# Shared-expert weights laid out ahead of the kernel, first rows and order table fetched early, and softmax of the routing scores moved to tiles 8 and 10

## The chip, the core and the metric

The kernel runs on one core of a Trainium2 chip. The metric is device time in microseconds (us) for one execution. The engines are TensorE (PE in the rows; PEld is its weight load), VectorE (DVE), ScalarE (ACT), GpSimd (POOL) and SyncE (SP), whose queue issues most DMAs. A granted clock of 1.00 is 2.4 GHz on TensorE, 0.5 is 1.2 GHz.

## The reference

The input is x [16, 256, 512] with a context of the same shape. The first layer multiplies the normalised x with the context in groups of 8 heads, runs a causal long convolution over the last axis, adds a skip term, multiplies with the context and sums. The second layer is a mixture of 64 experts, 6 per token, plus a shared expert.

```python
kv = vr[:, :, :, None, :] * x2r[:, :, None, :, :]
y = irfft(rfft(kv, n=2*L) * rfft(k, n=2*L))[..., :L] + kv * skip
x = x + einsum("bhijl,bhil->bhjl", y, x1r)
scores = softmax(xf @ gate_w.T)                 # xf is layernorm(x), 4096 tokens x 512
topk_w, topk_idx = top_k(scores, 6)             # each expert keeps its first 128 tokens
eo = (silu(g) * u) @ down_proj[e] * weight      # g, u = split(gx @ gate_up_proj[e])
shared = silu(xf @ sh_gate.T) * (xf @ sh_up.T) @ sh_down.T
x = x + routed + shared
```

## The kernel before

**Part A, 32 convolution tiles** (h = 0 to 31, 128 rows each). GpSimd forms the products (`product`, L1059) and their low halves (`low_part`, L1067), ScalarE the high halves (L809) and the filter blocks `toep` (L796 and L797, from `gr`, which SP loads from the DRAM tensor `filters`). TensorE convolves (`conv`, L445 to L449). VectorE multiplies the result with the context (`times`, L1221), sums it (`total`, L1227), and adds the residual (`add_x1`, L1255). Then come the second norm (`apply2` on ScalarE, L819), its transpose (`turn_xn`, L462) and the router (`router`, L468), the maximum, shifted scores and the mask of six experts (`experts_marked`, L1285; `experts_mask`, L837). These trail a tile or two behind the convolution. The transposed rows go to DRAM as `xT_rows`.

**Part B, 22 tiles of the shared expert** (t = 0 to 21). SP fetches transposed rows into `xn` (`b_load_xT`, L359), ScalarE copies them to the high half (`b_evacuate`, L903), VectorE forms the low half (`b_rows_low`, L1396). TensorE then runs two groups of 12 matmuls (`b_half`, L569: gate and up), three transposes (`b_turn_hid`, L580) and nine matmuls (`b_out`, L587). ScalarE takes the Silu (`b_gate`, L909) and evacuates the hidden rows (`b_evacuate_hid`, L915), VectorE makes `b_hidden` (L1409), `b_hidden_low` (L1401) and `b_result` (L1416). In tiles 2 to 17 VectorE also carries one round each of a search for the 128 first tokens of every expert: `first_best` (L1371) and `first_out` (L1376) over the table `place`. `place` is the DRAM constant `order` (1 MB, L389) times the turned expert masks (`places` on TensorE, L557, and `order_places` on VectorE, L1362). The weights of the first four routed experts are fetched in tiles 2 to 5.

**Part C, 64 routed experts**, with the ten remaining shared tiles spread among them. GpSimd gathers rows of `xn_rows`, whose last 64 columns are the routing probabilities, and adds results into the output.

**Handover from A to B.** The shared weights come from DRAM as they are. TensorE turns them in 11 pieces (`turn_weights`, L485 and L491), ScalarE and VectorE split each piece into high and low (L847, L1291). Four pieces stand inside the last convolution tile, seven behind it. There too stand the exponentials of all scores (L939, L945), their sums (L1445), the reciprocals and the multiplication (L1452), after which GpSimd writes the probabilities by 16 DMAs of 64 KB in pieces of 256 bytes (L1133).

Each engine runs its own instruction list in the order written. Waits are on semaphores.

## Time and profile before

| | |
|---|---|
| median of 3 runs | 1164.33 us (1163.23 to 1167.55) |
| the profiled execution | 1165.01 us, of which 1163.1 us is the span in the profile |
| TensorE busy | 1088.9 us, 94% |
| VectorE busy | 840.0 us, 72% |
| ScalarE busy | 526.9 us, 45% |
| GpSimd busy | 709.4 us, 61% |
| mean granted clock | 0.976 |

Busy shares are means over the three parts, which have different limits. The stretches matter more: A ends at about 548 us, B at about 724 us.

### The profile page before, as it was taken

To read this page: it belongs to the slowest core of one execution; us is meant where nothing else is said; L and a number is where in the kernel's file an instruction comes from. 1 tells how busy PE (TensorE), PEld (TensorE's weight loads), DVE (VectorE), ACT (ScalarE), POOL (GpSimd) and SP (SyncE) were. 2 spreads that over 40 slices of the span, in tenths; PEclk is the share of its full clock that TensorE was granted. 3 is DMA by queue.
4 is the path that set the end of the run, shared out by engine and by line. 5 is a ranking of instruction groups with operands and counts; after the bars stand their busy time and mean duration, and the time that the engine had idled before them with its cause. 6 is when DMAs were issued, how large, how long until landed. Compare 5 with 4: busy or idle time off the path is not lost. (4 is left out here: it accounts for less than half of the span.)

```text
span 1163.1 us, 17622 instructions
## 1 busy us (share of the span) xinstructions
PE 1088.9 (94%) x5113; PEld 852.8 (73%) x5113; DVE 840.0 (72%) x1444; ACT 526.9 (45%) x958; POOL 709.4 (61%) x414
## 2 busy tenths in 40 slices
PE   3999999999999999999689999999999899999973
PEld 2778777877778777787578889777777667777642
DVE  3799999999999999998579994456556455565533
ACT  5565556555665556553412222444444344444421
POOL 6999999999999999993210000154444353443623
PEclk9999999999999999999889999999999989999986
DMA  6365554455445554452485444599999999999984
GB/s 181 104 186 159 166 142 139 145 158 166 130 134 157 164 150 135 141 150 73 123 222 160 122 115 120 179 286 279 289 290 294 284 234 286 276 282 291 291 210 52
DMA packets 92029, 217.08 MB, mean 187 GB/s; under 512 B 11239, under 2 KB 16167, under 8 KB 91856
## 3 DMA queue, kind: packets, MB, share of 16 engines
q1 hardware_dynamic: 75440, 177.75, 50.3%
q0 software_dynamic: 16544, 38.78, 15.9%
q8 instruction: 22, 0.36, 0.1%
q14 instruction: 23, 0.19, 0.0%
HBM read 164.82 MB, written 52.18 MB: 187 GB/s over the span
## 5 line engine op out<-in xcount | busy, mean ns | idle before, releaser
L1059 POOL TENSOR_TENSOR ring<-vT,pT 128x1024 f32<-128x1024 f32 x128 | 249.1, 1956 | 9.5 <-ACT vT L803 9.5
L445 PE MATMUL Y<-split,toep 128*128 128x512 f32 x576 | 238.4, 414 | 11.5 <-ACT toep L797 9.4
L1067 POOL TENSOR_TENSOR split<-ring,split 128x1024 fp32r<-128x1024 f32 x96 | 230.8, 2404 | 1.6 <-ACT split L809 1.6
L447 PE MATMUL Y<-split,toep 128*128 128x512 f32 x576 | 227.4, 395 | 0.0
L446 PE MATMUL Y<-split,toep 128*128 128x512 f32 x576 | 226.2, 393 | 0.0
L689 PE MATMUL Y<-ring,xT 128*128 128x384 f32 x512 | 193.1, 501 | 0.8 <-DMA ring<-in_L_ffn_down_proj_dram 0.8
L1221 DVE TENSOR_TENSOR z<-Y,cT 128x1024 f32<-128x1024 f32 x128 | 157.0, 1227 | 26.5 <-PE Y L449 25.4
L1106 POOL DMA_INDIRECT stage<-xn_rows,idx_i x64 | 75.7, 1183 | 161.9 <-issue 161.6
L1227 DVE TENSOR_REDUCE o<-z 128x128 f32<-128x1152 f32 x128 | 172.2, 1345 | 1.2
L445 PEld LDWEIGHTS Y<-split,toep 128*128 128x128 f32 x576 | 109.1, 189 | 31.6 <-issue 10.3
L809 ACT ACTIVATE split<-ring 128x1024 fp32r<-128x1024 f32 x96 | 100.8, 1050 | 57.9 <-POOL ring L1059 57.9
L447 PEld LDWEIGHTS Y<-split,toep 128*128 128x128 f32 x576 | 108.7, 189 | 24.2
L446 PEld LDWEIGHTS Y<-split,toep 128*128 128x128 f32 x576 | 109.4, 190 | 19.8 <-issue 0.5
L689 PEld LDWEIGHTS Y<-ring,xT 128*128 128x128 f32 x512 | 88.9, 194 | 39.9 <-issue 2.1
L569 PE MATMUL Y<-split 128*128 128x384 f32 x528 | 105.4, 349 | 4.5 <-DVE split L1291 4.5
L569 PEld LDWEIGHTS Y<-split 128*128 128x128 f32 x528 | 95.4, 195 | 6.7 <-DVE split L1291 3.1
L1516 DVE TENSOR_TENSOR split<-TB,split 96x256 fp32r<-96x256 f32 x64 | 26.9, 420 | 100.6 <-ACT split L1004 98.8
L1127 POOL DMA_INDIRECT out_dram<-o,idx_i x16 | 25.9, 1617 | 106.2 <-DVE o L1561 55.3
L1127 POOL DMA_INDIRECT out_dram<-w,idx_i x16 | 25.7, 1606 | 99.3 <-DVE w L1561 38.8
L986 ACT ACTIVATE xT<-TA 128x512 f32<-128x512 f32 x64 | 37.6, 588 | 68.4 <-PE TA L677 68.4
L449 PE MATMUL Y<-ring,toep 128*128 128x512 f32 x128 | 65.3, 591 | 0.0
L903 ACT ACTIVATE split<-xn 128x512 fp32r<-128x512 f32 x32 | 20.2, 631 | 82.8 <-DMA xn<-xT_rows 76.7
(167 smaller groups left out, 1905.1 us busy)
## 6 DMA issues: line engine op xcount, KB each, us to landing
ring<-_L_ffn_gate_up_proj_dram SPq DMA_DIRECT2D x64, 768.0 KB, 6.8
ring<-in_L_ffn_down_proj_dram SPq DMA_DIRECT2D x64, 384.0 KB, 8.9
gr<-filters SPq DMA_DIRECT2D x32, 512.0 KB, 4.0
stage<-in_x_dram SPq DMA_DIRECT2D x32, 256.0 KB, 5.4
pT<-in_turned_dram SPq DMA_DIRECT2D x32, 256.0 KB, 4.2
cT<-in_turned_dram SPq DMA_DIRECT2D x32, 256.0 KB, 4.2
xr<-in_x_dram SPq DMA_DIRECT2D x32, 256.0 KB, 3.7
xn_rows<-xn SPq DMA_DIRECT2D x32, 256.0 KB, 2.9
```

Of the source, the lines that this page charges most:

```text
L445: pe.matmul(y, high, kv[:, s, 0, a, n], start=(a == 0), stop=False)
L446: pe.matmul(y, high, kv[:, s, 1, a, n], start=False, stop=False)
L447: last = pe.matmul(y, low, kv[:, s, 0, a, n], start=False, stop=(a == c))
L449: last = pe.matmul(y, toep0[:, s, :], kv3[s][:, n], start=False, stop=True)
L569: last = pe.matmul(Y[2 * s + g][:, 0:SI], xTs[:, s, a, c, :], sh_gu[:, b, c, g * SI:(g + 1) * SI], start=(c + a + b == 0), stop=(c == NC - ...
L689: last = pe.matmul(Y[s][:, 0:SI], xT[:, s, c, :], ring[:, r, c * SI:(c + 1) * SI], start=(c == 0), stop=(c == NC - 1))
L809: act.activation(kv[:, s, 0, c, :], kvp[c], ACT.Copy).then_inc(kv_high, 1)
L1059: pool.tensor_tensor(to.rearrange("p (b j i) -> p b j i", i=NH, j=NH), a, d, ALU.mult).then_inc(kvp_ready, 1)
L1067: pool.tensor_tensor(kv[:, s, 1, c, :], kvp[c], kv[:, s, 0, c, :].bitcast(F32), ALU.subtract).then_inc(kv_ready, 1)
L1106: pool.indirect_dma_start(out=xg[r], out_offset=None, in_=xn_rows, in_offset=bass.IndirectOffsetOnAxis(ap=idx_i[:, e:e + 1], axis=0),).the ...
L1221: dve.tensor_tensor(zz[c % 2][:, :, :, 0:NH], YY[c % 2][:, :].rearrange("p (b j i) -> p b j i", j=NH, i=NH), m, ALU.mult).then_inc(z_done, 1)
L1227: dve.tensor_reduce(o[:, s, c, :], z[:, c % 2, :].rearrange("p (n i) -> p n i", i=NH + 1), AX.X, ALU.add).then_inc(o_done, 1)
```

## The change

1. **Weights laid out.** The host function `shared_rows` lays the three shared matrices out in the transposed order. The 11 turns on TensorE are gone, with the 11 ScalarE and 11 VectorE pieces. In their place ScalarE makes three copies of 128x1536 (`shared_high`), GpSimd two subtractions of 128x1536 after its last product, and VectorE one (`shared_down_low`).
2. **First rows and order early.** Rows of tiles 0 and 1 of B go into `pT`, free after the last product, and not into `xn`. The order table is issued before the last stores. `places` writes TA and DX, no longer OT and DX. TensorE runs three tiles' halves while the last tile's norm, router and mask proceed.
3. **Other first instructions.** SP issues x first and `load_filter(0)` ahead of four tile transfers. ScalarE takes a square root of a constant first.
4. **Softmax later.** One exponential over all scores stands on ScalarE after tile 8, between two loops. The sums and the multiplication stand on VectorE in tile 10, which carries no round of the search. The search thus ends in tile 18.

```diff
+GATE_AT = 10
...
+        PL = [TA, DX]
...
+        shared = [ring[:, n, 0:n_up * L] for n in range(3)]
+        shared_to = [[sh_gu[:, a, :, g * SI:(g + 1) * SI] for a in range(2)] for g in range(2)]
+        shared_to.append([sh_d[:, a, :, :] for a in range(2)])
+
+        def shared_from(n):
+
+            return shared[n].rearrange("p (c i) -> p c i", c=n_up if n == 2 else NC)
+
+        def b_rows(t, s):
+
+            return pT[:, s, :, :].rearrange("p c n -> p (c n)") if among(t, 0, 1) else xn[:, s, :]
...
+            load_rows(0, 0)
             sp.dma_start(kin, k).then_inc(k_in, 16)
-            load_rows(0, 0)
             sp.dma_start(sq[:], c_sq).then_inc(consts_in, 16)
+            load_paired(0, 0)
+            sp.dma_start(skip_c[:].rearrange("p h i -> p (h i)"), bass.AP(skip.tensor, skip.offset, [[0, P], [1, D]])).then_inc(skip_in, 16)
             sp.dma_start(gate_in[:], gate_w).then_inc(gate_w_in, 16)
-            sp.dma_start(skip_c[:].rearrange("p h i -> p (h i)"), bass.AP(skip.tensor, skip.offset, [[0, P], [1, D]])).then_inc(skip_in, 16)
             sp.wait_ge(k_high, 1)
             sp.wait_ge(k_low, 1)
             for part in range(2):
                 sp.dma_start(filters[:, part, :], kparts[part].bitcast(F32)).then_inc(filters_out, 16)
             sp.dma_start(filters[:, 2, :], kpad).then_inc(filters_out, 16)
-            load_paired(0, 0)
             load_turned(0, 0)
             load_rows(1, 1)
+            sp.wait_ge(filters_out, 48)
+            load_filter(0)
             load_paired(1, 1)
             load_turned(1, 1)
             load_residual(0, 0)
             load_residual(1, 1)
             sp.dma_start(slot_c[:], c_slot).then_inc(small_in, 16)
-            sp.wait_ge(filters_out, 48)
-            load_filter(0)
...
+            sp.dma_start(shared[0], shared_rows[0]).then_inc(shared_in, 16)
...
                 if among(t, 0, 1):
-                    sp.wait_ge(xT_ps, NT - 1 + t)
+                    sp.wait_ge(kvp_ready, (NT - 1 + t) * NC)
+                elif among(t, 2, 3):
+                    sp.wait_ge(xT_ps, NT - 3 + t)
                     sp.wait_ge(xn_out[s], NT // 2 * 16)
                 else:
                     sp.wait_ge(b_xT_lo, t - 1)
                 sp.wait_ge(xT_out[s], landed(t, s, 16))
-                sp.dma_start(xn[:, s, :], xT_rows[t]).then_inc(b_xT_in[s], 16)
+                sp.dma_start(b_rows(t, s), xT_rows[t]).then_inc(b_first_in[s] if among(t, 0, 1) else b_xT_in[s], 16)
...
+            for t in range(2):
+                b_load_xT(t, t)
             store_xT(NT - 2, 0)
-            b_load_xT(0, 0)
+            b_load_xT(2, 0)
+            sp.wait_ge(z_done, NC * NT)
+            sp.wait_ge(o_done, NC * NT)
+            sp.dma_start(place, c_order).then_inc(order_in, 16)
             store(NT - 1, 1, late=True)
-            b_load_xT(1, 1)
             for t in range(2):
                 b_load_x1(t, t)
             store_xT(NT - 1, 1)
+            b_load_xT(3, 1)
...
+            b_iteration(0, 0, fetch_xT=False)
+            b_iteration(1, 1, fetch_xT=False)
+            sp.wait_ge(sh_lo, 2)
+            sp.wait_ge(sh_d_lo, 1)
...
-                else:
-                    pe.wait_ge(term_ready, NT)
-                    pe.wait_ge(xT_sb, NT - 2)
-                    turn_weights(0)
...
-                if among(h, NT - 1):
-                    turn_weights(1)
...
+                    last = pe.matmul(PL[g % 2][:, n * P:(n + 1) * P], mask[:, 2 * m:2 * m + 2, :], ident16[:],
...
-            for n in range(4, 7):
-                turn_weights(n)
-            turn_weights(7)
+            pe.wait_ge(z_done, NC * NT - 1)
+            pe.wait_ge(b_xT_lo, 1)
+            pe.wait_ge(sh_lo, 1)
+            b_half(0, 0, 0)
             turn_o(NT - 1, 1)
-            turn_weights(8)
-            pe.wait_ge(b_xT_lo, 1)
-            pe.wait_ge(sh_lo, 2 * NC)
-            b_half(0, 0, 0)
+            pe.wait_ge(sh_lo, 2)
+            b_half(0, 0, 1)
+            pe.wait_ge(z_done, NC * NT)
+            pe.wait_ge(b_xT_lo, 2)
+            b_half(1, 1, 0)
             pe.wait_ge(xT_sb, NT - 1)
             turn_xn(NT - 1, 1)
-            b_half(0, 0, 1)
+            b_half(1, 1, 1)
             pe.wait_ge(sc_ready, NT - 1)
             router(NT - 1, 1)
-            turn_weights(9)
-            turn_weights(10)
+            b_turn_hid(0, 0)
+            pe.wait_ge(b_xT_lo, 3)
+            pe.wait_ge(b_hid, 1)
+            b_half(2, 0, 0)
             places(0)
             places(1)
-            pe.wait_ge(b_xT_lo, 2)
-            b_half(1, 1, 0)
+            pe.wait_ge(x1_ready, NT)
+            pe.wait_ge(sh_d_lo, 1)
+            b_out(0, 0)
+            b_turn_hid(1, 1)
+            b_half(2, 0, 1)
             places(2)
-            b_turn_hid(0, 0)
-            pe.wait_ge(sh_lo, n_turn)
-            b_half(1, 1, 1)
             places(3)
-            pe.wait_ge(place_sb, 3)
-            b_out(0, 0)
-            b_iteration(2, 0)
+            pe.wait_ge(place_sb, 4)
+            b_out(1, 1)
             with pe.Fori(0, 9) as i:
...
+            act.wait_ge(dve_setup, 2)
+            act.activation(sd2[:], eps[:], ACT.Sqrt)
...
                 if n == 0:
+                    act.wait_ge(shared_in, 48)
                     act.wait_ge(conv_done, NC * (NT - 1))
-                if n == 2 * NC:
-                    act.wait_ge(conv_done, NC * NT)
-                act.activation(part[:, 0, :], bank, ACT.Copy).then_inc(w_sb, 1)
+                act.activation(shared_to[n][0], shared_from(n), ACT.Copy).then_inc(sh_hi, 1)
...
-            for n in range(3, 7):
-                shared_high(n)
             act.wait_ge(conv_done, NC * NT)
             b_evacuate(0, 0)
-            shared_high(7)
+            b_evacuate(1, 1)
+            keep_scores(NT - 2)
             sqrt2(NT - 1)
             apply2(NT - 1, 1)
-            keep_scores(NT - 2)
-            shared_high(8)
+            experts_mask(NT - 2)
             evacuate_xn(NT - 1, 1)
-            experts_mask(NT - 2)
-
-            act.wait_ge(sc_kept, NT - 1)
-            most, last = sc_all[:, 0:NT - 1, :], sc_all[:, NT - 1:NT, :]
-            act.activation(most, most, ACT.Exp).then_inc(exp_ready, 1)
-            b_evacuate(1, 1)
-            shared_high(9)
+            b_gate(0, 0)
+            b_gate(1, 1)
             keep_scores(NT - 1)
             experts_mask(NT - 1)
-            act.wait_ge(sc_kept, NT)
-            act.activation(last, last, ACT.Exp).then_inc(exp_ready, 1)
-            b_gate(0, 0)
-            shared_high(10)
             b_evacuate(2, 0)
             b_evacuate_hid(0, 0)
-            b_gate(1, 1)
             b_iteration(2, 0)
-            with act.Fori(0, NB // 2 - 2) as i:
+            with act.Fori(0, 3) as i:
+                b_iteration(i * 2 + 3, 1)
+                b_iteration(i * 2 + 4, 0)
+            act.wait_ge(sc_kept, NT)
+            act.activation(sc_all[:], sc_all[:], ACT.Exp).then_inc(exp_ready, 1)
+            with act.Fori(3, NB // 2 - 2) as i:
                 b_iteration(i * 2 + 3, 1)
                 b_iteration(i * 2 + 4, 0)
             b_iteration(NB - 1, 1)
...
+            for n in range(2):
+                pool.wait_ge(sh_hi, n + 1)
+                pool.tensor_tensor(shared_to[n][1], shared_from(n), shared_to[n][0].bitcast(F32),
+                                   ALU.subtract).then_inc(sh_lo, 1)
...
-                else:
-                    shared_low(0)
...
-                if not nxt:
-                    shared_low(1)
...
+            b_rows_low(0, 0)
             best_logit(NT - 2)
             total(NT - 1, 1, 3)
             scores(NT - 2)
-            for n in range(4, 7):
-                shared_low(n)
-            b_rows_low(0, 0)
-            shared_low(7)
+            b_rows_low(1, 1)
             add_x1(NT - 1, 1)
-            best_scores(NT - 2)
             stats2(NT - 1, 1)
             mean2(NT - 1)
+            best_scores(NT - 2)
+            six_scores(NT - 2)
             rstd2(NT - 1)
-            six_scores(NT - 2)
             shift2(NT - 1)
             experts_marked(NT - 2)
-            shared_low(8)
+            shared_down_low()
+            b_hidden(0, 0)
             best_logit(NT - 1)
             scores(NT - 1)
             best_scores(NT - 1)
             six_scores(NT - 1)
             experts_marked(NT - 1)
-            b_rows_low(1, 1)
-            shared_low(9)
-
-            dve.wait_ge(exp_ready, 2)
-            dve.tensor_reduce(sums[:], sc_all[:], AX.X, ALU.add).then_inc(sums_ready, 1)
-            dve.wait_ge(sums_ready, 1)
-            dve.reciprocal(rinv[:], sums[:]).then_inc(rinv_ready, 1)
+            b_rows_low(2, 0)
+            b_hidden(1, 1)
+            b_hidden_low(0, 0)
             order_places(0)
-            b_hidden(0, 0)
             order_places(1)
-            dve.wait_ge(rinv_ready, 1)
-            dve.tensor_tensor(sc_all[:], sc_all[:], rinv[:].unsqueeze(2).to_broadcast([P, NT, E]),
-                              ALU.mult).then_inc(prob_ready, 1)
-            shared_low(10)
-            b_rows_low(2, 0)
+            b_result(0, 0)
             order_places(2)
-            b_hidden_low(0, 0)
             order_places(3)
-            b_hidden(1, 1)
-            b_result(0, 0)
...
+                if among(t, GATE_AT):
+                    gate_sums()
...
+                if among(t, GATE_AT):
+                    gate_weights()
...
-            for n in range(NF):
-                b_iteration(n + 2, n % 2, n)
-            for t in range(MOVE_AT, NB):
-                b_iteration(t, t % 2)
+            for t in range(2, NB):
+                n = t - 2 - (t > GATE_AT)
+                b_iteration(t, t % 2, n if t != GATE_AT and n < NF else None)
...
+    up_parts = [a.reshape(SI, P, NC).transpose(1, 2, 0).reshape(P, NC * SI) for a in (gate, up)]
+    down_part = down.T.reshape(SI // P, P, L).transpose(1, 0, 2).reshape(P, SI // P * L)
+    return np.stack(up_parts + [down_part])
```

The first place is SP's queue at the start. `stage` is x, `z` the filter's input k, `pT` and `cT` two copies of the context, `xr` the residual. Before:

```order
L278 DMA z<-in_L_xattn_k_dram 32x512
L255 DMA stage<-in_x_dram 128x1x512
L280 DMA sq<-in_sq_dram 128x256
L281 DMA gate_in<-in_L_ffn_gate_w_dram 64x512
L282 DMA skip_c<-in_fside_S_0_dram 128x256
L286 DMA filters<-split 32x640 x2
L287 DMA filters<-z 32x640
L265 DMA pT<-in_turned_dram 128x512
L260 DMA cT<-in_turned_dram 128x512
...
L276 DMA xr<-in_x_dram 128x1x512 x2
L295 DMA slot_c<-in_slot_dram 128x1
L270 DMA gr<-filters 128x2x512
```

The same queue after the change:

```order
L260 DMA stage<-in_x_dram 128x1x512
L284 DMA z<-in_L_xattn_k_dram 32x512
L285 DMA sq<-in_sq_dram 128x256
L270 DMA pT<-in_turned_dram 128x512
L287 DMA skip_c<-in_fside_S_0_dram 128x256
L288 DMA gate_in<-in_L_ffn_gate_w_dram 64x512
L292 DMA filters<-split 32x640 x2
L293 DMA filters<-z 32x640
L265 DMA cT<-in_turned_dram 128x512
L260 DMA stage<-in_x_dram 128x1x512
L275 DMA gr<-filters 128x2x512
```

The load of `gr` moved ahead of `pT`, `cT` and both `xr`, and `pT` of tile 0 ahead of the filter stores.

The second place is TensorE from the last router of part A to the first `b_out`. `Y0` and `Y1` are the two-bank PSUM tiles, `xT` and `gateT` belong to the router. Before:

```order
L468 MATMUL DX<-gateT,xT 128x64 x4
L485 MATMUL Y0<-sq,ring 128x128 x6
L485 MATMUL TB<-sq,ring 128x128 x3
L485 MATMUL Y1<-sq,ring 128x128 x3
L456 MATMUL OT<-sq,o 128x128 x4
L491 MATMUL Y1<-sq,ring 128x128 x4
L569 MATMUL Y0<-split 128x384 x12
L462 MATMUL TA<-sq,xn 128x128 x4
L569 MATMUL Y0<-split 128x384 x12
L468 MATMUL DX<-gateT,xT 128x64 x4
...
L587 MATMUL OT<-split 128x512 x9
```

After the change:

```order
L475 MATMUL DX<-gateT,xT 128x64 x4
L539 MATMUL Y0<-split 128x384 x12
L463 MATMUL OT<-sq,o 128x128 x4
L539 MATMUL Y0<-split 128x384 x12
L539 MATMUL Y1<-split 128x384 x12
L469 MATMUL TA<-sq,xn 128x128 x4
L539 MATMUL Y1<-split 128x384 x12
L475 MATMUL DX<-gateT,xT 128x64 x4
L550 MATMUL TB<-sq,cT 128x128 x3
L539 MATMUL Y0<-split 128x384 x12
...
L557 MATMUL OT<-split 128x512 x9
```

The seven weight turns are gone, and four halves stand ahead of the second router where there were two.

The third place is ScalarE after tile 8, where the second loop of part B begins (`split<-xn` is `b_evacuate`, `vT<-Y` is `b_gate`, `split<-TB` is `b_evacuate_hid`). After the change:

```order
L915 ACT_TABLE_LOAD
L915 ACTIVATE sc_all<-sc_all 128x2048 [waits sc_kept]
L916 UNCONDITIONAL_BRANCH
L916 ISA
L873 REGISTER_ALU [waits b_xT_in0]
L874 ACT_TABLE_LOAD
L874 ACTIVATE split<-xn 128x512 [waits up_ps]
L877 REGISTER_ALU
L880 ACT_TABLE_LOAD [waits b_hid]
L880 ACTIVATE vT<-Y 128x384 [waits gate_ps]
L885 REGISTER_ALU [waits b_hT_ps]
L886 ACTIVATE split<-TB 128x384 [waits b_down]
```

Two loads of the activation tables now stand inside the body of the second loop, which runs seven times (two tiles each). The loop of the kernel before has none.

## Rows read from the trace of the kernel before

**Rows 1.** Windows: us, busy PE PEld DVE ACT POOL, PEclk, DMA share, GB/s
```profile
548.00:588.00 40.00, 28.06 (x159) 25.15 (x159) 26.30 (x46) 15.07 (x27) 10.78 (x16) 0.87 0.47 114
...
622.00:698.00 76.00, 74.04 (x398) 67.52 (x397) 71.71 (x76) 16.37 (x33) 0.00 (x0) 1.00 0.41 114
...
724.00:1163.00 439.00, 404.56 (x1784) 292.52 (x1783) 227.19 (x418) 174.69 (x328) 186.30 (x138) 0.96 0.91 254
```

**Rows 2.** Timeline of the start: start us, us, engine, operation, [idle before, releaser]
```profile
6.63 1.28 ACT L785 ACT_TABLE_LOAD   x1
...
11.39 3.85 POOL L1059 TENSOR_TENSOR ring<-vT,pT 128x1024 f32<-128x1024 f32 x2 [0.91 <-ACT vT L803]
...
18.75 0.31 ACT L796 ACTIVATE toep<-gr 128x128 f32<-128x128 f32 x1 [3.62 <-DMA gr<-filters]
...
21.10 2.37 POOL L1067 TENSOR_TENSOR split<-ring,split 128x1024 fp32r<-128x1024 f32 x1 [1.65 <-ACT split L809]
...
29.01 0.50 PE L445 MATMUL Y<-split,toep 128*128 128x512 f32 x1 [1.39 <-POOL split L1067]
```

**Rows 3.** Timeline of TensorE, routers that end tiles 29, 30 and 31
```profile
513.89 1.00 PE L468 MATMUL DX<-gateT,xT 128*128 128x64 f32 x8
...
530.23 1.00 PE L468 MATMUL DX<-gateT,xT 128*128 128x64 f32 x8
...
547.62 1.00 PE L468 MATMUL DX<-gateT,xT 128*128 128x64 f32 x8
```

**Rows 4.** Timeline of the handover from A to B
```profile
547.82 1.23 DVE L1221 TENSOR_TENSOR z<-Y,cT 128x1024 f32<-128x1024 f32 x1 [1.43 <-PE Y L449]
...
553.00 0.68 DVE L1255 TENSOR_TENSOR stage<-OT,xr 128x512 f32<-128x512 f32 x1
...
553.23 2.35 PE L569 MATMUL Y<-split 128*128 128x384 f32 x12 [1.65 <-DVE split L1291]
...
555.57 1.29 ACT L819 ACTIVATE xn<-stage,nb,rs 128x512 f32<-128x512 f32 x1 [0.48 <-DVE nb L1212]
...
559.55 1.00 PE L468 MATMUL DX<-gateT,xT 128*128 128x64 f32 x8
...
562.08 0.21 DVE L1285 MATCH_REPLACE8 marked<-s,sc 128x66 f32<-128x66 f32 x1
...
564.46 3.64 PE L569 MATMUL Y<-split 128*128 128x384 f32 x12
...
570.34 0.69 DVE L1362 TENSOR_TENSOR z<-z,OT 128x512 f32<-128x512 f32 x1 [3.24 <-DMA z<-in_order_dram]
...
585.77 2.24 PE L587 MATMUL DX<-split 128*128 128x512 f32 x9
```

**Rows 5.** Timeline of tiles 2 to 6 of part B
```profile
592.71 0.63 ACT L903 ACTIVATE split<-xn 128x512 fp32r<-128x512 f32 x1 [8.28 <-DMA xn<-xT_rows]
...
596.87 4.18 PE L587 MATMUL OT<-split 128*128 128x512 f32 x9 [4.33 <-DVE split L1401]
...
606.20 2.24 PE L587 MATMUL DX<-split 128*128 128x512 f32 x9
...
619.96 2.21 PE L587 MATMUL DX<-split 128*128 128x512 f32 x9
```

**Rows 6.** Timeline: the exponentials' table load, and a steady tile of B
```profile
558.43 1.28 ACT L939 ACT_TABLE_LOAD   x1
...
559.72 1.86 ACT L939 ACTIVATE sc_all<-sc_all 128x1984 f32<-128x1984 f32 x1
...
621.80 0.63 ACT L903 ACTIVATE split<-xn 128x512 fp32r<-128x512 f32 x1 [3.19 <-DMA xn<-xT_rows]
...
623.55 0.68 DVE L1396 TENSOR_TENSOR split<-xn,split 128x512 fp32r<-128x512 f32 x1
```

**Rows 7.** GpSimd's low parts (groups by line), and its DMAs' share in 545 to 615 us
```profile
L1067 POOL TENSOR_TENSOR split<-ring,split 128x1024 fp32r<-128x1024 f32 x96 | 230.8, 2404 | 1.6 <-ACT split L809 1.6
...
q0 software_dynamic: 768, 1.07, 12.7%
```

110 lines of the change are left out of this document (33 added, 77 removed).

## Prediction

> **What bounds the kernel now.** I read the page first, then the windows by stage, then the timeline at the seams. In part B's steady stretch TensorE is busy 74.0 of 76 us and VectorE 71.7 of 76 [rows 1]: TensorE paces it, VectorE is 3% behind. In part C the DMA engines are 91% busy at 254 GB/s [rows 1]. That stage starts when the token list is there, so whatever is saved before it moves it forward one for one. The poor stretch is 548 to 588 us: TensorE is busy 28.1 of 40 us, at a granted clock of 0.87 [rows 1]. The timeline says why. TensorE's first half of part B starts at 553.23, behind weight turns; the adder of the last residual, ready behind VectorE's weight pieces, runs at 553.00; the order table holds VectorE until 570.34, where its queue, `b_hidden` included, stands behind `order_places` [rows 4]. I call the end of the last convolution e = 547.8 (VectorE's last `times` starts at 547.82). The second `b_out` ends at 585.77 + 2.24 = 588.0, which is e + 40.2 [rows 4].
>
> **The start, -2.7 us.** GpSimd's chain sets it: TensorE waits at 29.01 for GpSimd's third low part [rows 2]. Two things leave that chain. The table load of 1.28 us ahead of the first product goes to time zero, but the filter's input k now lands behind x and the constant's square root stands ahead, for which I give back 0.3: -1.0. GpSimd's wait of 1.65 us at 21.10 was on a ScalarE copy, which stood behind a wait of 3.62 us for the filter load [rows 2]. That load now goes ahead of four transfers, so the wait should vanish: -1.65. Queued behind SP's earlier wait on the filter stores are `pT` and `cT` of tile 1, both residuals and tile 2, all needed a tile later. Bounds: -0.5 (x and k late) to -4.9 (1.28 + 3.62, if everything follows ScalarE).
>
> **Tile 31, -1.8 us.** Routers start at 513.89, 530.23 and 547.62: a usual tile takes 16.34, the last 17.39 [rows 3], although it turns no next tile. The four weight turns fill that. Without them I expect about 15.6, since the missing turn of v is worth some 0.7 of the 16.34. Bounds: -1.0 (VectorE becomes the later one) to -2.4. The three new ScalarE copies stand where six waits on TensorE stood. GpSimd's two subtractions cost 3.6 us each (2.404 us for 1024 columns [rows 7], times 1.5). They are covered by its idle time: behind its last low part it has nothing but the 16 DMA issues (10.78 us [rows 1]). Uncovered, they would hold the second half until e + 7.2, some 2 us.
>
> **The handover, -9.7 us.** Followed by row durations from e. `times` 1.23 and `b_rows_low` 0.68 end at e + 1.9 (tile 0's rows are fetched while tile 31 runs). The half of 2.35 us ends at e + 4.3. Turning o, two halves, turning the normed rows, one half and the router come to some 9.5 (three halves of 2.35, three short groups of 0.6 to 1.0): e + 13.8. Beside it runs the norm: from 553.00 to 555.57 + 1.29 it took 3.9 us [rows 4], so rows that are added at e + 5.1 are normed at e + 9.0, before TensorE asks. From the router's end (559.55 + 1.00) to the marks (562.08 + 0.21) there were 1.7 us. Now ScalarE's mask, its copy for tile 2 (0.63) and `b_rows_low` (0.68) follow, so the next half starts at e + 17.2. That is a TensorE gap of some 2.5 us, after a turn of the hidden rows. After such a gap the half took 3.64 us instead of 2.35, and the nine matmuls at 596.87, after 4.33 us of waiting, 4.18 instead of 2.21 [rows 4, 5], so I charge 3.64: e + 20.9. `places` twice 0.8, `b_out` 2.24, turn and half 3.0, `places` with two multiplications of 0.69 in turn 1.4, `b_out` 2.24: e + 30.5 against 40.2. The order table is issued at e + 3.5 and had 8 us to land before; it is needed at e + 21. Bounds: -5 (one more wait of the size of VectorE's 3.24 us for that table, with its clock loss) to -13 (no gap).
>
> **Tiles 2 to 5, -5.2 us.** Between 588.0 and the `b_out` that ends at 619.96 + 2.21 = 622.2 lie four tiles in 34.2 us. Steady, two tiles take 619.96 - 606.20 = 13.76, so four 27.5 [rows 5]. The excess is the 8.28 us wait for rows fetched at 592.71 and its echo [rows 5]. That fetch met the weights of the first routed experts and GpSimd's probability writes, which filled 12.7% of 70 us of the 16 engines, 8.9 us [rows 7]. The writes are gone from there, the weights not: I allow 1.5 us, 29.0. Bounds: 0 (the weights did it) to -6.7.
>
> **What is added, +3.0 us.** (a) The search ends a tile later, 17 loaded tiles for 16. TensorE lacks 76 - 74.04 us over 11 tiles, 0.2 each [rows 1], and the tile with sums and multiplication carries a reciprocal besides: together 0.5. The list is still made in tile 21. (b) The 8.9 us of probability writes now meet tile 10's transfers. Bounds 0 to 8 (two late fetches of 4 us). The load there is only 114 GB/s [rows 1], so I take 1.5. (c) The exponential, 1.28 + some 1.9 us [rows 6], fits ScalarE's 3.19 us of waiting for rows at 621.80. (d) The order of the changed kernel shows two table loads inside the second loop, seven passes, 14 loads of 1.28 us. The first stands behind the wait for the rows. In a steady tile the copy would end at 621.80 + 1.28 + 0.63 = 623.71, VectorE took it at 623.55 [rows 6]: 0.2 us late in the five passes with search, 1.0 in all. The second lies between copy and Silu, where ScalarE waits for TensorE. Without that cover: 2.56 less the slack of 623.55 - 622.43 = 1.1, seven times, 10 us.
>
> The Trainium skill, "ScalarE: Activation LUTs", section "What ACT_TABLE_LOAD costs", puts a switch at 1283 ns of load plus about 1380 ns of drain, 2.66 us. The row shows the load's 1.28, with the exponential starting right behind it at 559.72 [rows 6]. By the page's figure the copy would come 1.5 us late in seven passes, an estimate of 11 us, and the sum would end near 1158; I go by the row.
>
> **Sum.** -2.7 - 1.8 - 9.7 - 5.2 + 3.0 = -16.4. Against the profiled execution (1163.1 of span plus 1.9 around it, 1165.0) that gives 1148.6; the median of the runs stands 0.7 lower: 1147.9, rounded to 1148.
>
> **Rivals.**
> - *The handover keeps a wait* (0.09). The late fetches, the mask or a subtraction holds TensorE once more, with clock loss. For it: every wait there is on a chain of four engines. Against: nothing long is ahead of `b_hidden` now. Handover and tiles 2 to 5 then bring half, 7.5 less: 1155.
> - *More than forecast* (0.08): no low clock, no cost of the writes, full gain at the start: 1148 less 13, 1131 to 1139.
> - *Table loads on the path* (0.06): 10 us, less the 1.0 in the sum: 1157. The drain of the page would act so.
> - *Slower* (0.03): the same loads, and TensorE falls to the low clock in each of the seven passes. Then each costs 1.4 + 1.97 (4.18 less 2.21) + 1.29 (3.64 less 2.35) = 4.7 us, 33 in all: 1180. It decides from 2.5 us per pass (17.4 over 7). Against it: the steady clock is 1.00 and the loads' gap is 0.2 us by the rows.
> - *No effect* (0.02): the gain is given back before part C, for instance by a token list held by the probabilities; they are written some 80 us before it.
>
> **How the numbers follow.** The forecast holds 0.72, within 1139 to 1157 by the terms' bounds when not all fall on one side; with parts of the first and third rival the range holds 0.8. About 0.5% (5.8 us) is what a measurement of this kernel tells from no change. Faster: 0.72 + 0.09 + 0.08 + 0.03 = 0.92. Same: 0.03 + 0.02 = 0.05. Slower: 0.03.
>
> **What would show it.** Start: TensorE's wait for the third low part ends near 26.3, none of GpSimd's on ScalarE's second copy. Last router some 15.6 after the one before, e near 543.3. Second `b_out` ended by e + 31, its successors 6.9 apart, no wait of 4 us on rows. In tiles 9 to 21 VectorE's `b_rows_low` waits 0.2 us on ScalarE every second tile; waits of over 1 us there would make me wrong, as would late fetches in tile 10 for longer than two tiles, or a gap of over 5 us ahead of the third half.

## The result, and the profile after

The changed kernel takes 1161.66 us (median of 20 runs, 1156.45 to 1164.32); the kernel before takes 1164.88 in the same job (20 runs, 1162.47 to 1171.65). The ratio of the two is 0.9953, with a 95% interval of 0.9937 to 0.9968. It is faster by 3.2 us in the medians and 5.5 in the ratio, where 17 were forecast: the direction was right, the size was not, and 1161.66 lies above the range. The profiled execution spans 1161.0 us, against 1163.1 before.

The windows, which answer to [rows 1], show the handover denser and the steady stretch of part B thinner. Part C follows; its loss is taken up at the end. Columns as in [rows 1].

```profile
546.00:586.00 40.00, 32.72 (x176) 29.82 (x177) 26.66 (x43) 9.97 (x19) 0.00 (x0) 0.91 0.53 163
622.00:698.00 76.00, 68.61 (x358) 62.21 (x357) 64.35 (x68) 27.11 (x40) 10.79 (x16) 0.98 0.47 117
715.00:1161.00 446.00, 407.20 (x1785) 293.71 (x1783) 227.24 (x418) 175.10 (x328) 188.11 (x138) 0.95 0.90 250
```

In the 40 us of the handover TensorE is busy 32.7 instead of 28.1 us. In 622 to 698 it is busy 68.6 of 76 instead of 74.0. That is where an added cost sits that the forecast had put too low.

The timelines of the start and of the last routers answer to [rows 2, 3]. TensorE's wait for the third low part ends at 26.73 instead of 29.01, and tile 31 takes 543.82 - 527.98 = 15.84 instead of 17.39.

```profile
18.84 2.37 POOL L1031 TENSOR_TENSOR split<-ring,split 128x1024 fp32r<-128x1024 f32 x1
...
26.73 0.50 PE L452 MATMUL Y<-split,toep 128*128 128x512 f32 x1 [2.44 <-POOL split L1031]
...
527.98 1.00 PE L475 MATMUL DX<-gateT,xT 128*128 128x64 f32 x8
...
543.82 1.00 PE L475 MATMUL DX<-gateT,xT 128*128 128x64 f32 x8
```

The handover answers to [rows 4]; e is now 544.02.

```profile
545.94 2.33 PE L539 MATMUL Y<-split 128*128 128x384 f32 x12 [1.12 <-DVE z L1189]
...
555.37 1.00 PE L475 MATMUL DX<-gateT,xT 128*128 128x64 f32 x8
...
559.69 3.77 PE L539 MATMUL Y<-split 128*128 128x384 f32 x12 [2.62 <-DVE split L1355]
...
563.89 2.33 PE L557 MATMUL OT<-split 128*128 128x512 f32 x9
...
573.60 3.88 PE L557 MATMUL DX<-split 128*128 128x512 f32 x9 [4.51 <-DVE split L1360]
```

The first half ends at e + 4.3, the router at e + 12.4 (forecast e + 13.8), and behind it comes the gap of 2.6 us with tile 2's half of 3.77, which ends at e + 19.4 (forecast e + 20.9). What was not forecast is the last row. The second `b_out` waits 4.51 us and ends at e + 33.5, not e + 30.5. VectorE says what it waits for:

```profile
569.52 0.68 DVE L1321 TENSOR_TENSOR z<-z,DX 128x512 f32<-128x512 f32 x1
570.12 0.69 DVE L1355 TENSOR_TENSOR split<-xn,split 128x512 fp32r<-128x512 f32 x1
570.72 2.29 DVE L1330 MAX8 w<-z 128x8 f32<-128x2048 f32 x1
572.92 0.54 DVE L1360 TENSOR_TENSOR split<-TB,split 128x384 fp32r<-128x384 f32 x1
```

`b_hidden_low(1)` (L1360) takes what ScalarE copied from 566.58 to 567.07, 5.9 us before it starts, but stands behind the last `order_places`, tile 3's rows and the first MAX8.

The rows of tiles 13 and 14 come late. ScalarE's copy waits 6.78 and then 7.62 us for them, where [rows 6] had 3.19, beside the 16 probability writes on GpSimd. TensorE then waits behind VectorE, ahead of the `b_out` of tiles 11 and 12 (the expectations below call them 10 and 11):

```profile
643.25 0.63 ACT L874 ACTIVATE split<-xn 128x512 fp32r<-128x512 f32 x1 [6.78 <-DMA xn<-xT_rows]
...
652.26 1.28 ACT L874 ACT_TABLE_LOAD   x1 [7.62 <-DMA xn<-xT_rows]
653.55 0.63 ACT L874 ACTIVATE split<-xn 128x512 fp32r<-128x512 f32 x1
...
634.58 10.79 POOL L1101 DMA_DIRECT2D xn_rows<-sc_all  x16 [95.95 <-DVE sc_all L1418]
...
647.42 2.31 PE L557 MATMUL DX<-split 128*128 128x512 f32 x9 [2.74 <-DVE split L1360]
...
657.72 2.89 PE L557 MATMUL OT<-split 128*128 128x512 f32 x9 [3.46 <-DVE split L1360]
```

**One table for all profiles.** Each kernel below left one profile. The columns are differences of start times on VectorE: `b_result` of tile 1, then from tile 1 to 5, 5 to 9, 9 to 13 and 13 to 21, then the start of `b_result(21)`. After that comes part C, from the first expert's `c_hidden` to the last one's, and in it the stretch from expert 29 to 33. The last column is the median of all runs of that kernel. The kernels ran in six jobs, and the kernel before had medians from 1164.48 to 1165.92 in them; each kernel's ratio is to the kernel before of its own job. So two versions are better compared by the difference of their ratios (0.001 is 1.2 us) than by their medians, and their intervals are 2 to 4 us to either side.

```
kernel           y1      1-5    5-9    9-13   13-21  y21     C       29-33  median
before           588.76  34.19  27.52  27.49  51.51  729.47  402.94  34.28  1164.88
before_again     588.30  34.06  27.52  27.49  51.48  728.85  406.08  37.25  1164.93
smalladd_before  587.59  31.26  30.66  27.51  51.48  728.50  383.46  24.95  1147.55
after            577.52  28.21  27.96  35.26  51.62  720.57  409.26  39.19  1161.66
after_again      578.22  28.87  28.19  35.72  51.58  722.58  410.06  39.43  1162.25
delay8           577.58  28.43  27.99  34.24  51.51  719.75  407.21  37.67  1166.82
delay21          575.97  27.72  28.02  33.06  51.78  716.55  408.95  37.84  1181.70
smalladd_after   577.92  30.62  28.40  33.43  51.99  722.36  386.50  24.77  1146.23
oldstart         580.62  30.99  28.28  36.00  51.54  727.43  403.77  35.49  1160.36
early            578.54  34.17  27.52  27.51  51.58  719.32  403.67  33.64  1158.75
peel             577.96  28.26  27.46  33.23  51.47  718.38  404.76  35.91  1157.47
hidlow           574.74  27.90  27.74  33.81  51.76  715.95  402.04  32.79  1155.75
peel_hid         574.96  32.23  27.44  34.07  51.52  720.22  404.72  34.57  1154.65
spread           579.31  27.87  28.14  30.30  60.59  726.21  403.90  35.13  1162.46
twice            579.41  27.92  28.16  36.83  56.68  729.00  414.09  37.35  1165.25
spwrites         577.60  28.82  27.80  29.36  55.48  719.06  410.76  40.54  1159.13
hid_all          576.57  31.95  30.88  35.81  53.85  729.06  407.28  39.33  1163.32
best             576.41  28.95  27.46  27.94  52.40  713.16  403.13  33.06  1149.13
best_all         576.23  27.79  29.11  27.39  51.27  711.79  404.75  35.25  1150.93
```

The first three rows run the same part B as the kernel before, the next five that of the changed kernel. Their means give what the change does up to the end of part B: y1 588.22 to 577.44 (-10.8), tiles 1 to 5 33.17 to 28.77 (-4.4), 5 to 9 -0.5, 9 to 13 27.50 to 34.34 (+6.8), 13 to 21 +0.2, in all 728.94 to 720.36, -8.6. One of the three traces of part B before (smalladd_before) has its late row behind tile 5 and not ahead of it. Against the two others alone tiles 1 to 5 give -5.4 and tiles 5 to 9 +0.6, with the same sum. So 8.6 of the forecast 16.4 are there when part C starts, and 3.2 to 5.5 at the end.

### The profile page after: what moved, and what is told of

The parts are those of the page before. It is cut to its first block and busy times, and to the rows that moved or that the text cites. A ratio compares the mean times of both kernels' runs of the same rounds, so it can differ in the third digit from the quotient of the medians.

```text
span 1161.0 us, 17543 instructions
## 1 busy us (share of the span) xinstructions
PE 1086.6 (94%) x5077; PEld 849.0 (73%) x5077; DVE 836.5 (72%) x1434; ACT 541.0 (47%) x961; POOL 718.2 (62%) x416
## 5 line engine op out<-in xcount | busy, mean ns | idle before, releaser
L659 PE MATMUL Y<-ring,xT 128*128 128x384 f32 x512 | 196.0, 507 | 0.4 <-DMA ring<-in_L_ffn_down_proj_dram 0.4
L659 PEld LDWEIGHTS Y<-ring,xT 128*128 128x128 f32 x512 | 90.4, 197 | 40.5 <-issue 4.2
L1101 POOL DMA_DIRECT2D xn_rows<-sc_all x16 | 10.8, 717 | 96.0 <-DVE sc_all L1418 96.0
```

Source lines behind the costliest of these rows:

```text
L659: last = pe.matmul(Y[s][:, 0:SI], xT[:, s, c, :], ring[:, r, c * SI:(c + 1) * SI], start=(c == 0), stop=(c == NC - 1))
```

## The experiments

### What part C does with an earlier or later start

**delay8** puts additions on GpSimd ahead of the first gather:

```diff
+            for n in range(7):
+                pool.tensor_tensor(w[:, 0, :], zeros[:, 0:L], zeros[:, 0:L], ALU.add).then_inc(delayed, 1)
+                pool.wait_ge(delayed, n + 1)
             for e in range(NG - 2):
                 fetch(e)
```

> The changed kernel with seven additions of 128 x 512 zeros on GpSimd between the token list and the first gather of part C, some 8 us by GpSimd's rate in this trace (2.404 us for 1024 columns). Theory A (part C absorbs an earlier start: it is held by its transfers from about expert 30 on, so a later start costs less than itself): the first gather moves by about 8, the end by only 2 to 4 us, so the time is 1164 to 1166. Rival B (part C starts when the list is there and every us ahead of it counts; that the gain of the changed kernel vanished at experts 30 and 60 is chance): the end moves by 8, the time is about 1169 to 1170.

Measured: 1166.82 us, 5.2 above the changed kernel's median; the ratio to the kernel before is 1.0008 (0.9985 to 1.0031), 0.0055 or 6.4 us above that of the changed kernel. In the trace the first gather comes 7.8 us later than `b_result(21)` would have it, and the first expert 6.5. The medians lie between the two theories, the ratio near B. So the lever was made longer.

**delay21** is the same with `range(21)`.

> The changed kernel with 21 additions instead of 7 ahead of the first gather of part C: 21.0 us by the 7.0 that the seven took. Theory A (part C absorbs): the time rises by less than 17, below 1179. Theory B (one for one, the rest is chance in the stalls near experts 30 and 60): the time rises by 21 plus some 0.5 for a low clock behind the wait, to 1181 to 1184.

Measured: 1181.70 us, 20.0 above; ratio 1.0144 (1.0112 to 1.0176), 22.3 above the changed kernel's.

```profile
709.93 23.70 POOL L1109 TENSOR_TENSOR w<-zeros 128x512 f32<-128x512 f32 x21 [66.54 <-DVE idx_i L1355]
734.57 1.07 POOL L1075 DMA_INDIRECT stage<-xn_rows,idx_i  x1 [0.94 <-POOL w L1109]
```

The additions take 23.7 us, not 21, so the first expert is some 23 us late and the kernel 20 to 22 (the changed kernel in the same job, after_again below: 1162.25). Theory A falls: part C does not give a shifted start back. Of the forecast's premise the part "moves it forward one for one" holds.

**before_again** and **after_again** are second profiles of the two kernels, unchanged.

> The kernel before once more, for a second profile of it. Theory A (the stalls of part C are chance): from its first gather to the last expert part C takes anything between 415 and 423 us, as in six profiles of changed versions. Rival B (part C of the changed kernel is slower by itself, by some 3 to 4 us): it takes 416 again, and its stall near expert 60 stays at 37.9, below all those of the changed versions (38.5 to 40.7).

> The changed kernel once more, for a second profile of it. By chance in part C: it takes 415 to 422 us from the first gather to the last expert instead of the first profile's 423.0; the first gather lies between 714 and 717; the profiled span is 1152 to 1160. If part C of this kernel is slower by itself, it takes 422 to 424 again.

Measured: 1164.93 us, ratio 0.9990 (0.9973 to 1.0007), for the first; 1162.25, ratio 0.9959 (0.9930 to 0.9988), for the second. From first gather to last expert before_again takes 419.2 us and after_again 423.2, against 416.1 and 423.0 in the first profiles. The kernel before thus varies by 3 us, as chance would have it; the changed one repeated its long value, against what I expected of chance. Its first gather (716.8) was as expected, its span (1163.2) was not. Experts 0 to 29 take 175.6 to 175.7 us in 16 of the 19 profiles; the differences arise near experts 30 and 60.

**smalladd_before** and **smalladd_after** cut the accumulated tiles of part C to 8 of 128 rows:

```diff
-                    pool.dma_start(rows(out[0:T, :], t), y2[(t - NB) % NY2], accum_op=ALU.add).then_inc(y2_added, 16)
+                    pool.dma_start(rows(out[0:T, :], t)[0:1], y2[(t - NB) % NY2][0:NH], accum_op=ALU.add).then_inc(y2_added, 16)
```

> The kernel before with each of the ten accumulated tiles of part C (256 KB from GpSimd's queue) cut to 8 of its 128 rows, so that the output of those tiles lacks the shared experts in the other rows. Theory A (these two bursts of five tiles are what stalls TensorE near experts 30 and 60, and the stalls vary from run to run and hide the changed kernel's gain): the stall of 13 to 18 us between two c_out near expert 30 vanishes, the kernel ends 5 to 12 us earlier, and the changed kernel cut in the same way ends 8 to 9 us ahead of this one, as its first gather does. Rival B (part C as a whole runs at the rate of its transfers): the difference of the two stays near 3 us.

> The changed kernel cut in the same way (8 of 128 rows of each accumulated tile, the shared experts are missing from the other rows). Theory A: 8 to 9 us ahead of the kernel before cut so. Rival B: 3 us ahead, and TensorE waits for gathers or weights in other places of part C instead.

Measured: 1147.55 and 1146.23 us, ratios 0.9855 (0.9829 to 0.9881) and 0.9850 (0.9818 to 0.9882). Experts 29 to 33 take 24.8 to 25.0 us instead of 32.8 to 40.5, so the burst of five accumulated tiles is what stalls them. In the whole kernel the wait is VectorE's, for the adds of an earlier pair that queue behind the burst. Before ("o<-DX" is the copy of an expert's result):

```profile
929.45 0.69 DVE L1547 COPY o<-DX 128x512 f32<-128x512 f32 x1 [6.65 <-DMA out_dram<-o,idx_b]
```

After:

```profile
924.96 0.69 DVE L1509 COPY o<-DX 128x512 f32<-128x512 f32 x1 [10.49 <-DMA out_dram<-o,idx_b]
```

The second half of theory A was not confirmed: cut, the changed kernel is 1.3 us ahead in the medians, with intervals wide enough for 0 and for 5; in the profiled pair the spans are 1146.2 and 1141.0. Even with the burst cut, part C of the changed kernel is 3.0 us longer (386.50 against 383.46), nearly all of it in the last five experts.

### The start

**oldstart** undoes the first instructions only (cut to its core):

```diff
-            act.wait_ge(dve_setup, 2)
-            act.activation(sd2[:], eps[:], ACT.Sqrt)
...
-            load_rows(0, 0)
             sp.dma_start(kin, k).then_inc(k_in, 16)
+            load_rows(0, 0)
...
             sp.dma_start(slot_c[:], c_slot).then_inc(small_in, 16)
+            sp.wait_ge(filters_out, 48)
+            load_filter(0)
```

> The changed kernel with SyncE's and ScalarE's first instructions as before: k ahead of x, the filter load behind the loads of tile 1 and both residuals, no square root of the constant first. By the term of the forecast and the traces TensorE's wait for the third low part ends at 29.0 instead of 26.7, the first gather comes 2.3 us later (717 to 719), and the time is about 2.3 higher than the changed kernel's in the same job.

Measured: TensorE's wait for the third low part ends at 29.52 us, 2.8 and 2.4 later than in the two profiles of the changed kernel (26.73, 27.11), and GpSimd's wait on ScalarE is back:

```profile
21.63 2.37 POOL L1029 TENSOR_TENSOR split<-ring,split 128x1024 fp32r<-128x1024 f32 x1 [2.32 <-ACT split L779]
...
29.52 0.50 PE L452 MATMUL Y<-split,toep 128*128 128x512 f32 x1 [2.29 <-POOL split L1029]
```

`b_result(1)` comes 3.2 us later than the mean. The median, 1160.36, ratio 0.9962 (0.9943 to 0.9981), does not show it: the changed kernel in the same job has 1162.25 and 0.9959, and a shift of 2.4 us is below what these intervals tell. The expected 2.3 us in the time were not seen; those in the trace were.

### The handover

**hidlow** moves the low part of tile 1's turned hidden rows ahead of the first MAX8:

```diff
-                if first is not None:
+                if first is not None and not among(t, 2):
                     first_best(first)
...
                 b_hidden_low(t - 1, 1 - s)
+                if among(t, 2):
+                    first_best(first)
```

> The changed kernel with VectorE's low part of tile 1's turned hidden rows ahead of the first MAX8 search round instead of behind it. Theory: TensorE's wait of 4.51 us before the second b_out (573.60) shrinks by the 2.29 us of the MAX8, and the second b_out ends at e + 31, the first gather comes 2 to 3.5 us earlier. Rival (VectorE is behind anyway, and the MAX8 round only moves): b_out of tile 1 is earlier but tile 2's hidden rows are later by the same, and nothing is left at the fifth b_out.

Measured: 1155.75 us, ratio 0.9922 (0.9894 to 0.9950): 5.9 us below the changed kernel in the medians, 3.6 in the ratios. The wait falls from 4.51 to 2.32 us. The granted clock over the nine matmuls is 1.00 instead of 0.54, and they take 2.32 instead of 3.88.

```profile
570.05 2.32 PE L557 MATMUL DX<-split 128*128 128x512 f32 x9 [2.32 <-DVE split L1360]
```

Against the means y1 is 2.7 us earlier and `b_result(5)` 3.6, so the gain is kept in this trace, and the theory stands for the wait. It is not kept in every trace: peel_hid and best (below) carry the same edit, and there a later row is late in tiles 2 to 5, so that `b_result(5)` comes at 607.2 and 605.4, where the means of the changed kernel give 606.2.

**hid_all** does the same in every tile:

```diff
-                if first is not None:
-                    first_best(first)
...
                 b_hidden_low(t - 1, 1 - s)
+                if first is not None:
+                    first_best(first)
```

> The changed kernel with the low part of the turned hidden rows ahead of the MAX8 in every tile, not only in tile 2. Theory (a late row costs TensorE 2.3 us more than its lateness, because MAX8 stands between the row's low part and the hidden rows' low part, so the probability writes and table loads are dear only through that order): b_result 9 to 13 falls from 33 to 37 us to 29 to 32, the first gather comes at 706 to 709, time 1150 to 1154. Rival (hidden_low now waits for ScalarE's copy and holds MAX8 back, VectorE becomes the bound): steady tiles take more than 6.9 us, b_result 5 to 9 more than 28.5, time above 1158.

Measured: 1163.32 us, ratio 0.9996 (0.9972 to 1.0019), and 9 to 13 takes 35.81. The theory falls, and what the rival named is there: tiles 5 to 9 take 30.88 us, and the first of them, 8.59 us, ends before the table load of the exponential. MAX8 now stands behind two waits on ScalarE, and in every second tile of the second loop the copy of the hidden rows comes a table load after the copy of the rows as well.

```profile
658.48 0.63 ACT L874 ACTIVATE split<-xn 128x512 fp32r<-128x512 f32 x1
659.12 1.28 ACT L880 ACT_TABLE_LOAD   x1
660.42 0.49 ACT L880 ACTIVATE vT<-Y 128x384 f32<-128x384 f32 x1
660.81 0.48 ACT L886 ACTIVATE split<-TB 128x384 fp32r<-128x384 f32 x1
```

### What was added in part B

**peel** writes ScalarE's tiles 9 and 10 out behind the exponential:

```diff
-            with act.Fori(3, NB // 2 - 2) as i:
+            b_iteration(9, 1)
+            b_iteration(10, 0)
+            with act.Fori(4, NB // 2 - 2) as i:
```

> The changed kernel with ScalarE's tiles 9 and 10 of part B written out behind the exponential, so that the loop over the later tiles starts with the table it needs and holds no table load. Theory A (the 14 loads of 1.28 us are hidden but for the first copy after the probability writes): the first gather comes 0.5 to 2 us earlier. Rival B (the loads are what tiles 9 to 21 lost): the first gather comes 4 us or more earlier, and b_out of tile 10 and 11 no longer waits 2.7 and 3.5 us on VectorE.

Measured: 1157.47 us, ratio 0.9939 (0.9918 to 0.9960). In the trace the first gather comes 2.2 us earlier and the two late tiles stay, against rival B:

```profile
646.94 2.31 PE L557 MATMUL DX<-split 128*128 128x512 f32 x9 [2.32 <-DVE split L1362]
655.67 3.88 PE L557 MATMUL OT<-split 128*128 128x512 f32 x9 [1.89 <-DVE split L1362]
```

By the traces of peel and peel_hid tiles 9 to 13 take 33.65 instead of 34.34 us and 13 to 21 51.50 instead of 51.70: the loads cost 0.9 us, less than tiles 9 to 21 differ between traces of the changed kernel (84.8 to 87.3). The median is 4.2 lower, but the ratio only 1.6 us, which is within the intervals. The Trainium skill's figure ("ScalarE: Activation LUTs", section "What ACT_TABLE_LOAD costs"), by which the forecast had them at an estimate of 11 us, is not borne out: the rows of hid_all above show a load of 1.28 us that starts right behind the copy (658.48 + 0.63, load at 659.12), and the next instruction right behind the load (660.42).

**twice** issues the 16 probability writes a second time in tile 15:

```diff
-            for b in range(B):
...
+            for again in range(2):
+                if again:
+                    pool.wait_ge(prob_out, B * 16)
+                    pool.wait_ge(y_ready, GATE_AT + 5)
+                for b in range(B):
...
-            pool.wait_ge(prob_out, B * 16)
+            pool.wait_ge(prob_out, 2 * B * 16)
```

> The changed kernel with the 16 probability writes issued a second time in tile 15. Theory A (a burst of these writes makes the rows of two tiles late and costs some 5 us): the waits of 2 to 3.5 us on VectorE behind tiles 10 and 11 come again behind tiles 15 and 16, the first gather is 4 to 6 us later, the time 1165 to 1168. Rival B (the two late tiles come from the ends of the exponential and of the sums): no new wait, the time stays at 1162.

Measured: 1165.25 us, ratio 1.0000 (0.9983 to 1.0017), and tiles 13 to 21 take 56.68 instead of 51.70 us: one burst costs 5.0 (15 of its writes from 680.2 on, the last at 697.9), and the ratio is 5.5 us above that of the changed kernel. The profiled run is this kernel's slowest, 1175.83; its further excess sits in part C (414.09). Two tiles are late, one of them at a granted clock of 0.53 (3.88 us instead of 2.3):

```profile
692.14 3.88 PE L557 MATMUL OT<-split 128*128 128x512 f32 x9 [2.24 <-DVE split L1364]
701.97 2.31 PE L557 MATMUL DX<-split 128*128 128x512 f32 x9 [1.41 <-DVE split L1364]
```

**early** puts exponential, sums and gate weights back to the front, and with them the writes:

```diff
-GATE_AT = 10
+GATE_AT = 2
...
-            b_iteration(2, 0)
-            with act.Fori(0, 3) as i:
-                b_iteration(i * 2 + 3, 1)
-                b_iteration(i * 2 + 4, 0)
             act.wait_ge(sc_kept, NT)
             act.activation(sc_all[:], sc_all[:], ACT.Exp).then_inc(exp_ready, 1)
-            with act.Fori(3, NB // 2 - 2) as i:
+            b_iteration(2, 0)
+            with act.Fori(0, NB // 2 - 2) as i:
```

> The changed kernel with its second half undone: the exponential behind tile 1, sums and gate weights in tile 2, so that the search runs from tile 3 on, the probability writes meet the weights of the first experts as before, and the second loop has no table load. Theory A (the writes cost 6 to 7 us where they now stand, in tiles 9 to 13, and less beside the experts' weights, where rows were late anyway): b_result 9 to 13 takes 27.5 instead of 33 to 37 us, 1 to 5 to 5 to 9 together gains or loses at most 4, the second b_out comes 0 to 3 us later, and the time is 1157 to 1161. Rival B (moving them away was worth the 5.2 us and more that were forecast): tiles 2 to 5 take 34 us again, the second b_out comes 4 us later, the time is 1164 or more.

Measured: 1158.75 us, ratio 0.9951 (0.9934 to 0.9969). Tiles 1 to 5 take 34.17 instead of 28.77 us (+5.4), tiles 9 to 13 27.51 instead of 34.34 (-6.8), y1 is 1.1 later, and y21 is 1.0 earlier. Neither theory holds whole. Theory A has the time and tiles 9 to 13, but tiles 1 to 9 together lose 4.8 us where it allowed 4; rival B has tiles 2 to 5 at 34 us again, but not the 1164. The second half of the change thus moved a cost of 5 to 7 us from one place to another, and no gain is left of it (the ratios differ by 0.2 us, with an interval of some 3 to either side). In the front it looks just as in the later place:

```profile
589.76 0.63 ACT L874 ACTIVATE split<-xn 128x512 fp32r<-128x512 f32 x1 [7.27 <-DMA xn<-xT_rows]
...
577.65 10.78 POOL L1098 DMA_DIRECT2D xn_rows<-sc_all  x16 [38.53 <-DVE sc_all L1415]
```

**spread** issues the writes two at a time from GpSimd, a pair for each finished tile:

```diff
             for b in range(B):
+                if b and b % 2 == 0:
+                    pool.wait_ge(y_ready, GATE_AT + b // 2)
```

> The changed kernel with the 16 probability writes on GpSimd issued two at a time, one pair for each finished tile from tile 10 on, not all at once. Theory A (the burst of small writes makes the two fetches of rows for tiles 11 and 12 late, 7 to 8 us instead of 4, and that is most of the 7.7 us that tiles 6 to 21 lost, where 3.0 were forecast): TensorE's waits of 2.74 and 3.46 us behind tiles 10 and 11 vanish and the first gather comes 5 to 7 us earlier. Rival B (the table loads did it): the waits stay, the first gather moves by less than 1 us.

Measured: 1162.46 us, ratio 0.9983 (0.9960 to 1.0005). The two waits are gone, but four others of 1.7 to 2.5 us stand behind every second tile, and tiles 9 to 21 take 90.9 us against 86.0. Theory A holds for the two tiles and fails for the sum: spread over tiles with a table load, the same writes cost more. The fetches of rows land 5.2 us after their issue (median in 650 to 710 us), where they took 3.8 in the steady tiles of the kernel before.

**spwrites** lets SyncE issue them, behind the transfers of tiles 11 to 18:

```diff
-            with sp.Fori((2 + NW) // 2, MOVE_AT // 2) as i:
+            with sp.Fori((2 + NW) // 2, GATE_AT // 2) as i:
...
-            for t in range(MOVE_AT, NB):
+            for t in range(GATE_AT, NB):
...
+                if GATE_AT < t <= GATE_AT + B // 2:
+                    sp.wait_ge(prob_ready, 1)
+                    for b in range(2 * (t - GATE_AT) - 2, 2 * (t - GATE_AT)):
+                        sp.dma_start(xn_rows[b * D:(b + 1) * D, L:].rearrange("(h j) e -> j h e", j=NH),
+                                     sc_all[b * NH:(b + 1) * NH, :, :]).then_inc(prob_out, 16)
...
-            for b in range(B):
-                pool.dma_start(xn_rows[b * D:(b + 1) * D, L:].rearrange("(h j) e -> j h e", j=NH),
-                               sc_all[b * NH:(b + 1) * NH, :, :]).then_inc(prob_out, 16)
```

> The changed kernel with the probability writes issued by SyncE, two behind the transfers of each of tiles 11 to 18, in the queue of the rows and not on GpSimd's. Theory A (the fetches of rows are late because the small writes of another queue share the engines with them; behind them in one queue they are not): the four waits of 2.4 us of the spread version vanish, b_result 9 to 13 takes 28 to 29 us, the first gather comes 4 to 6 us earlier, the time 1156 to 1158. Rival B (4096 pieces of 256 bytes take the engines' time wherever they stand): the waits stay, 1160 to 1164.

Measured: 1159.13 us, ratio 0.9932 (0.9908 to 0.9955). The four waits shrink to 1.0 to 1.8 us and do not vanish; tiles 9 to 21 take 84.8 us, and the first gather comes 1.3 us earlier than the mean of the changed kernel, not 4 to 6. So neither theory holds whole. The fetches of rows now land in 4.0 us (median). Those four are the tiles with a table load between rows and copy.

### The edits together

**peel_hid** joins peel and hidlow.

> Both edits that gained alone: no table load in ScalarE's second loop, and the low part of tile 1's turned hidden rows ahead of the first MAX8. By the sum of the two apart (first gather 2.2 and 4.6 us earlier, medians 4.2 and 5.9 lower than the changed kernel's 1161.7) the first gather comes at about 708 and the time is 1152 to 1155. Rival (part C gives an earlier start back): the first gather comes at 708 and the time stays at 1156 to 1158.

Measured: 1154.65 us, ratio 0.9908 (0.9881 to 0.9936), as expected by the sum, although its profile shows a late row in tile 4 (tiles 1 to 5 in 32.23 us). In the ratios the two edits alone give 1.6 and 3.6 us and together 5.2.

**best** joins peel, hidlow and spwrites.

> Three edits together: no table load in ScalarE's second loop, low part of tile 1's hidden rows ahead of the first MAX8, probability writes issued by SyncE. If the writes' edit works alone, its 4 to 6 us add to the 10 of the other two by their medians apart: 1149 to 1152. If it does not, the time is that of the two edits, 1153 to 1156.

Measured: 1149.13 us, ratio 0.9875 (0.9849 to 0.9901). That is 15.8 us below the kernel before and 12.5 below the change in the medians, 14.6 and 9.1 in the ratios. Without table loads the pairs of writes are hidden: ScalarE waits 4.7 us for rows instead of 3.2, but in time, and TensorE hardly waits.

```profile
651.09 2.31 PE L562 MATMUL OT<-split 128*128 128x512 f32 x9 [0.33 <-DVE split L1364]
...
646.93 0.63 ACT L879 ACTIVATE split<-xn 128x512 fp32r<-128x512 f32 x1 [4.70 <-DMA xn<-xT_rows]
```

The window of the steady stretch is back at 74.0 of 76 us:

```profile
622.00:698.00 76.00, 73.98 (x394) 66.85 (x393) 65.99 (x72) 16.63 (x33) 0.00 (x0) 1.00 0.47 129
```

Tiles 9 to 21 take 80.3 us, where the changed kernel takes 86.0 and the one before 79.0. spwrites has 84.8, peel 84.7 and peel_hid 85.6: each edit alone gains 0.5 to 1.3 us, which is within the spread of the changed kernel's own traces, both together 5.7. No run has those two without hidlow's, which acts in tile 2. The times do not show more than a sum: in the ratios peel, hidlow and spwrites give 1.6, 3.6 and 2.4 us, together 7.6, against 9.1, and in the medians the sum is 12.6 against 12.5.

**best_all** is best with the order of hid_all.

> The same order in every tile, with no table load in ScalarE's second loop and the probability writes issued by SyncE. If what is left in the best version (1149) of waits behind MAX8 goes, the first gather comes 1 to 4 us earlier than 707.5 and the time is 1145 to 1149. If VectorE becomes the bound, it is 1150 or more.

Measured: 1150.93 us, ratio 0.9874 (0.9854 to 0.9894): no different from best. Tiles 9 to 21 take 78.7 us here, a second trace in which the writes cost next to nothing once the loads are gone.

## Why the prediction was wrong

Direction and most steps were right. The sum was too large by 7.8 us up to the end of part B, and by some 3 to 5 more behind it. Point by point, by its own terms:

- *The start, -2.7:* -2.3 in the first pair of profiles, -2.4 to -2.8 by oldstart. Right in its mechanism, 0.4 too large; GpSimd's wait on the second copy vanished.
- *Tile 31, -1.8:* -1.55. Right.
- *The handover, -9.7:* -6.7 in the profiled pair (588.0 - 577.48 = 10.5, less the two above). The failed step is "turn and half 3.0, `places` with two multiplications of 0.69 in turn 1.4, `b_out` 2.24: e + 30.5". I followed TensorE's queue to that `b_out` and not VectorE's, where `b_hidden_low(1)` stands behind MAX8. From the end of tile 2's half to the end of that `b_out` it took 14.0 us instead of 9.6; the half itself had ended 1.5 us earlier than forecast. hidlow gives 2.7 us back.
- *Tiles 2 to 5, -5.2:* -4.4 in the means (-5.4 without smalladd_before), and early prices it at 5.4. The reasoning, that the probability writes were what made rows late there, is shown by that run.
- *What is added, +3.0:* here a term was mis-sized. From tile 5 to 21 the traces show +6.6 in the means (+7.6 without smalladd_before). (d), the table loads at 1.0, measured 0.9 beside a single burst of writes. The second loop makes six passes, i = 3 to 8, and not seven as the description of the change and the forecast have it, and the trace has 12 loads in it, not 14; this changes the rivals' prices (10 us becomes 8.8, 33 becomes 28) and the estimate from the Trainium skill (11 becomes 9), not the 1.0, which counts five passes. (b), the writes at 1.5, measured 5.0 (twice) to 6.1 (peel and peel_hid against before): inside its own bounds of 0 to 8, but I took a value near the low end: "The load there is only 114 GB/s [rows 1], so I take 1.5." The mean load did not foretell it. The rows are fetched into two buffers, and both fetches that meet the burst are late in either place: in the trace of twice the two beside the first burst land 7.0 and 8.4 us after their issue, where 3.8 is usual. The row that should have set the value was the other term's: what the writes cost in tiles 2 to 5.
- *The premise,* that part C starts "when the token list is there, so whatever is saved before it moves it forward one for one". delay21 bears it out for a start that is moved, 20 to 22 of 23 us. Yet of the 8.6 us only 3.2 (medians) or 5.5 (0.9937 to 0.9968: 3.7 to 7.3) reach the end. Part C takes 409.3 and 410.1 us in the two profiles of the changed kernel, 402.9 and 406.1 in those of the one before. So the step "one for one" failed for the gain as a whole, by 3 to 5 us, and why it did stays open.

What lengthens part C is not settled. It sits near experts 30 and 60, behind the bursts of accumulated tiles, and is no matter of when part C starts: delay21 starts last and takes 409.0, hidlow starts early and takes 402.0. oldstart has the same code behind its first instructions as the changed kernel and takes 403.8, which speaks for chance; after_again repeated 39.4 us for experts 29 to 33, which speaks against. The five versions without table loads in the second loop lie at 403.1 to 404.8, the others with their loop at 402.0 to 414.1; no mechanism in part C links the two, and none is claimed.

Of the rivals, "the handover keeps a wait" (1155) named one of the two losses ahead of part C, though not the engine queue that caused it. "No effect" has the gain given back before part C by a held token list, which no trace shows. None put the writes higher, and none had a loss inside part C.
